# Decoder layer with two attentions on one core: full-width matmul pieces move ahead of the tiled ones in each attention step

## What is computed

```
x = layernorm(x + L0_attn(x))                    # 4 blocks of linear attention and feed-forward
x = layernorm(x + L0_xattn(x, ctx, mask))        # 16 heads of 8, masked softmax over 256 keys
x = layernorm(x + L0_ffn(x))
# L0_ffn: rmsnorm; rotary self-attention, 16 heads of 64, causal;
#         then one shared and 31 routed experts, the best 3 of 31 for each token
scores = where(mask, q k^T, -inf);  attn = softmax(scores);  ctx = attn @ v
```

## Time and profile before

| what | value |
| --- | --- |
| executions shown | 903.26, 904.5, 901.44 us |
| median | 903.26 us |
| span of the profiled execution, first to last instruction | 867.6 us |
| own time of the profiled execution | not shown apart; the median less the span is 35.7 us |
| TensorE busy | 796.4 us (92%), 5325 matmuls |
| VectorE busy | 692.1 us (80%) |
| ScalarE busy | 572.9 us (66%) |
| GpSimd busy | 562.2 us (65%) |
| mean granted TensorE clock | 0.982 |

### The profile page before, as it was taken

One profiled execution on the slowest core, in us unless ns is written; L12 is line 12 of the kernel. 1 busy time (PEld: TensorE's weight loads), 2 busy tenths in 40 slices (PEclk: granted clock), 3 DMA queues, 4 the chain that ended last, 5 costly groups with the idle time before them and its releaser, 6 DMA issues.

```text
span 867.6 us, 17391 instructions
## 1 busy us (share of the span) xinstructions
PE 796.4 (92%) x5325; PEld 525.5 (61%) x5325; DVE 692.1 (80%) x2494; ACT 572.9 (66%) x1445; POOL 562.2 (65%) x638
## 2 busy tenths in 40 slices
PE   5899999999889999999989999999999888989994
PEld 2344444444466676766546676676667556888773
DVE  4788888888788988889878859976995985565786
ACT  3588778777489999999656647645664656355334
POOL 4888888888662333232377749665788988663773
PEclk9799999999989999999999999999999999999997
DMA  8300000000015011100222222221222236264112
GB/s 242 116 2 0 1 1 0 1 0 1 0 36 153 30 42 56 39 1 2 50 65 68 65 50 51 68 65 40 63 76 77 54 93 195 91 191 146 50 49 61
DMA packets 57851, 51.88 MB, mean 60 GB/s; under 512 B 11586, under 2 KB 43042, under 8 KB 57762
## 3 DMA queue, kind: packets, MB, share of 16 engines
q1 hardware_dynamic: 55394, 46.05, 19.2%
q0 software_dynamic: 2304, 4.72, 1.9%
q10 hardware_dynamic: 64, 0.02, 0.0%
HBM read 21.66 MB, written 12.32 MB: 39 GB/s over the span
## 4 chain that ended last, share of the span: by engine, by line
PE 51%; POOL 19%; DVE 13%; issue 8%; ACT 7%; ACTq 0%; DVEq 0%; POOLq 0%
PE psum L2199 5%; PE psum L2028 4%; PE psum L2061 4%; POOL area L970 4%; DVE area L1482 4%; PE psum L2355 3%; PE psum L2336 3%; PE psum L2394 3%; PE psum L2258 3%; PE psum L2045 3%; POOL area L879 3%; PE psum L2087 3%; PE psum L2372 3%; POOL slot_in L958 2%; PE psum L1912 2%
## 5 line engine op out<-in xcount | busy, mean ns | idle before, releaser
L970 POOL TENSOR_TENSOR area<-area,rinv 128x512 f32<-128x512 f32 x64 | 94.2, 1472 | 64.7 <-DVE rinv L1803 64.3
L1275 ACT ACTIVATE area<-area,negmax 128x128 f32<-128x128 f32 (+1 forms) x256 | 112.8, 444 | 17.7 <-DVE negmax L1482 17.4
L1122 ACT ACTIVATE area<-area,negmax 128x256 f32<-128x256 f32 x256 | 108.9, 507 | 0.2
L1470 DVE SCALAR_TENSOR_TENSOR area<-psum,ccol,cs 128x512 f32<-128x512 f32 x128 | 89.4, 740 | 21.2 <-PE psum L2061 21.0
L1482 DVE CUSTOM_DVE_ANT_0 area<-psum,area 128x256 f32<-128x256 f32 x256 | 93.2, 420 | 14.4 <-PE psum L2013 13.9
L1482 DVE CUSTOM_DVE_ANT_0 area<-psum,maskc 128x128 f32<-128x128 f32 (+1 forms) x256 | 75.8, 351 | 10.0 <-PE psum L2087 10.0
L2028 PE MATMUL psum<-ident,area 128*128 128x128 f32 x512 | 70.9, 279 | 9.0 <-DVE area L1522 7.7
L2061 PE MATMUL psum<-area,qkw 128*128 128x512 f32 x128 | 71.9, 643 | 6.3 <-DVE area L1470 4.5
L2028 PEld LDWEIGHTS psum<-ident,area 128*128 128x128 f32 x512 | 57.3, 143 | 18.1 <-issue 11.3
L1265 ACT ACTIVATE area<-psum 128x512 f32<-128x512 f32 x32 | 19.1, 598 | 72.1 <-PE psum L2394 72.0
L2372 PEld LDWEIGHTS psum<-ident,area 128*128 128x128 f32 x384 | 44.8, 141 | 35.2 <-issue 24.9
(11 more groups left out here) (308 smaller groups left out, 2092.3 us busy)
## 6 DMA issues: line engine op xcount, KB each, us to landing
area<-area SPq DMA_DIRECT2D x256, 64.0 KB
slot_out<-area SPq DMA_DIRECT2D x17, 256.0 KB, 2.4
area<-slot_in SPq DMA_DIRECT2D x8, 512.0 KB, 4.0
slot_in<-gate SPq DMA_DIRECT2D x5, 768.0 KB, 4.6
area<-in_L_ffn_re_w SPq DMA_DIRECT2D x14, 256.0 KB, 3.4
area<-in_mask_BxSxS_ik SPq DMA_DIRECT2D x8, 256.0 KB, 3.8
area<-in_L_attn_W SPq DMA_DIRECT2D x5, 256.0 KB, 6.2
area<-in_x SPq DMA_DIRECT2D x4, 256.0 KB, 3.4
```

The costliest lines, as they stand in the source:

```text
L970: pool.tensor_tensor(p4, p4, rinv[:, u % 4, 0:4].unsqueeze(2).to_broadcast([128, 4, w]), ALU.mult)\
L1122: last = act.activation(P[:, n % 4, r, mm, :], P[:, n % 4, r, mm, :], ACT.Exp, bias=negmax[:, n % 4, r, mm:mm + 1], scale=-1.0)
L1275: last = act.activation(Pc[:, u % 4, r, mm, 0:w], Pc[:, u % 4, r, mm, 0:w], ACT.Exp, bias=negmax[:, u % 4, r, mm:mm + 1], scale=-1.0, accu ...
L1470: last = nc.vector.scalar_tensor_tensor(rp[:, w, j, :].rearrange("p (b n) -> p b n", b=2), src.rearrange("p (b n) -> p b n", b=2), ccol[:, ...
```

## The change: the order of three lists

On TensorE, in an odd step of the context attention, `values` moves from before the late and head pieces to the end of the step, so that the next step's scores come right behind. In a self-attention step the spare pieces move ahead of `self_scores`, so that `values` comes right behind the scores. On VectorE the reads of these spare pieces move ahead of `self_max` in the same way; the reads of `out`, `rank` and `base` stay behind it. ScalarE's, GpSimd's and SyncE's lists stay as they are, and no instruction is added or taken away. The hunks are VectorE's self-attention, TensorE's context attention and TensorE's self-attention.

```
@@ -1814,10 +1814,13 @@
                     if u == 1:
                         read_spare(g, steps[0], following)
+                    for step in steps:
+                        if step[0] in ("v", "logits", "pick", "b2") or step[0] == "tail" and step[1] in ("tokens0", "tokens1", "out"):
+                            read_spare(g, step, following)
                     if u < SU and (u + 2 < SU or following is not None):
                         self_max(g, u + 2)
                     for step in steps:
-                        if step[0] in ("v", "out", "logits", "rank", "base", "pick", "b2") or step[0] == "tail" and step[1] in ("tokens0", "tokens1", "out"):
+                        if step[0] in ("out", "rank", "base"):
                             read_spare(g, step, following)
@@ -2101,13 +2104,13 @@
-                if n % 2 and 0 <= n - 3 < XN:
-                    values((n - 3) // 2)
                 for what, b in fills(n, LATE):
                     fill_second(what, b)
                 for what, i in head(n):
                     pe.wait_ge(x_read, FILL[what, i])
                     fill_step(SPARE_FIRST[i], None, 0).then_inc(x_fill, 1)
+                if n % 2 and 0 <= n - 3 < XN:
+                    values((n - 3) // 2)
@@ -2411,11 +2414,11 @@
-                    if u < SU and (u + 2 < SU or following is not None):
-                        self_scores(g, u + 2)
                     for step in steps:
                         if step[0] not in ("half", "out", "rank", "base"):
                             fill_spare(g, step, following)
+                    if u < SU and (u + 2 < SU or following is not None):
+                        self_scores(g, u + 2)
                     if 2 <= u < SU + 2:
                         values(u - 2)
```

## The result

| | median, us | lowest to highest | runs |
| --- | --- | --- | --- |
| before | 903.89 | 899.74 to 908.75 | 22 |
| changed | 906.68 | 903.55 to 910.83 | 22 |

The changed kernel takes 1.0026 of the time before (95% interval 1.0013 to 1.0038): 2.3 us more by the ratio. It is slower, by little, though the interval lies clear of 1. The forecast, 898.1 us with a range to 904.0, is wrong in sign. The granted TensorE clock of the timed executions differs too: its mean is 0.962 for the 22 of the changed kernel, and 0.968 for 69 executions of before that stood beside later runs.

What follows compares the result with a forecast made beforehand. ScalarE was taken to bound mid context attention, TensorE the first self-attention group, VectorE the third. Terms -3.0 - 0.9 - 4.7 + 3.4 = -5.2 us, from 903.26, gave 898.1 us, 8-in-10 range 892.5 to 904.0.

Steps and rivals of the forecast that it cites:

- stage by stage reading: ScalarE fullest in mid context attention; self-attention: TensorE in first group (49.27 of 50 us), VectorE in third (47.87).
- reading of 35.7 us: Whole kernel: 35.7 us of a timed execution were taken to lie around the profiled span.
- Part 1: Middle context attention: `context` ahead of the values removes ScalarE's 1.00 us wait; 0.5 us a sequence, -3.0 us (0 to -6.0).
- Part 2: End of context attention: head pieces ahead of the values come 1.0 us earlier for VectorE; -0.9 us (0 to -1.2).
- Part 3: Self-attention: fewer tile-shape changes gain where TensorE is full; 2.2, 1.1, 1.0 and 0.4 by group, -4.7 us.
- price of a tile shape: TensorE, self-attention: each change of tile shape costs 0.19 us, and the new order saves one in a step.
- Part 4: Self-attention: a spare piece that waits now holds up the scores too; +3.4 us given back (0 to +5).
- rms: First self-attention group: this TensorE piece waits 0.73 us for GpSimd, with the scores now behind it; +0.55 us.
- turn: Router piece on TensorE, three groups: waits for VectorE's L1629 with the scores now behind; +0.6 us each, +1.9.
- gates: Second self-attention group: this TensorE piece waits for VectorE ahead of the scores; +0.35 us.
- logits: Router piece ahead of the scores, three groups: about 0.2 us absorbed in second and third, +0.6 in the last.
- VectorE waits for late scores: Rival, chance 0.10: self-attention `v` steps start scores 0.86 us later; 12 places costing that add 10.3 us, giving 908.

Runs made afterwards that it cites:

- context_only: Kernel before with only the context attention's part of the change: ratio 0.9969 to the kernel before, -2.7 us.
- v_heads_behind: Changed kernel with only `v` ahead in the self-attention, and the context attention's head pieces back behind the values: 902.78 us, ratio 0.9968 to before.
- turn_back: Changed kernel with the router's `turn` (three times) behind the scores again, on TensorE alone: ratio 0.9990 to before.
- unwaited_ahead: Changed kernel with `rms`, `turn`, `logits`, `gates` behind the scores again on TensorE, and `logits` behind the minima on VectorE: 901.51 us, ratio 0.9971 to before.
- v_only: Changed kernel with only `v` ahead in the self-attention, on TensorE and VectorE; context attention's part kept: 865.99 us, ratio 0.9953 to before, short chip.
- v_only_again: Same kernel as `v_only`, run again on the long chip: 901.3 us, ratio 0.9977 to before.
- after_again: The changed kernel run once more, nothing altered, on the long chip: 906.31 us, ratio 1.0024 to before.

## Why the prediction was wrong, step by step

The prediction failed in two steps: its gross gain, -8.6 us, was 3.9 too large (parts 1 to 3), and part 4 priced a wait only at the work that no longer hid in it.

**What bounds the kernel.** The stage by stage reading held, though the earlier trace rows, cited for the first group, are of the second. For the third group it says that what TensorE saves there doesn't count, and part 3 counts 1.0 us there all the same; the first was right. The reading of 35.7 us did not hold; it did no harm to the sum, which is a difference, but hid the fact that rows of a different chip were used.

**Part 1, right in mechanism, a third too large.** Forecast -3.0, 0.5 for each of six sequences. Measured over five sequences (from the third to the thirteenth L1144) 112.86 us against 114.68, 0.36 each, and -2.1 for the stage with its end. A sequence repeats every 22.57 us, above the 22.4 to 22.5 named as the sign of being right. The new wait on the values is 0.61 us; the prediction's own times (copy from 377.81, L1144 at 378.7) imply some 0.5, so 0.1 of the missing 0.14 lies there.

**Part 2, wrong.** Forecast -0.9, measured nothing from the heads, and from the thirteenth L1144 to the end of the stage 42.07 us against 41.80: +0.3, with +0.3 more in the next step. The failed step is "Ahead of them it comes 1.0 us earlier": VectorE's read of the half piece starts 31.3 us after the thirteenth L1144 in both orders, and its wait only shrinks from 1.92 to 1.81 us. In `context_only`, VectorE and then TensorE:

```profile
429.31 1.41 DVE L1470 SCALAR_TENSOR_TENSOR area<-psum,ccol,cs 128x512 f32<-128x512 f32 x2 [1.81 <-PE psum L2061]
```

```profile
428.14 1.13 PE L2061 MATMUL psum<-area,qkw 128*128 128x512 f32 x2 [0.82 <-ACT area L1110]
...
433.67 1.13 PE L2061 MATMUL psum<-area,qkw 128*128 128x512 f32 x2 [1.50 <-DVE area L1470]
```

The piece of the first row waits for ScalarE's copy in front of the values, and the next one for VectorE itself; the first starts 30.1 us after the thirteenth L1144 in both orders, the second 0.3 us later than before. The 0.3 us is not the heads' doing, for `v_heads_behind` has it too (42.14); what returns it was not tried.

**Part 3, gain of `v` right where TensorE is full, absent elsewhere.** The price of a tile shape was confirmed. A `v` step from the turn to the values, changed kernel and then before (short chip):

```profile
537.59 1.04 PE L2375 MATMUL psum<-ident,area 128*128 128x128 f32 x8
538.46 1.03 PE L2071 MATMUL psum<-vw,area 128*128 128x256 f32 x4
539.42 0.71 PE L2090 MATMUL psum<-area 64*128 64x128 f32 x8
540.07 0.66 PE L2397 MATMUL psum<-area 128*64 128x128 f32 x8
```
```profile
538.70 1.04 PE L2372 MATMUL psum<-ident,area 128*128 128x128 f32 x8
539.66 0.71 PE L2087 MATMUL psum<-area 64*128 64x128 f32 x8
540.31 1.13 PE L2068 MATMUL psum<-vw,area 128*128 128x256 f32 x4
541.37 0.66 PE L2394 MATMUL psum<-area 128*64 128x128 f32 x8
```

2.48 us instead of 2.67, so 0.19 saved as forecast, though L2071 itself takes 0.96 and not 0.87: the turn in front of it, 0.87 instead of 0.96, has the other tenth. Half of the 0.19 is the weight load, as the prediction had it: in before the first load of L2068 starts 0.11 us ahead of its product behind a full-width piece (425.96 and 426.07 us), and with it behind scores. The second group gains 1.0 us with `v` alone (forecast 1.1), the first 1.0 behind its second step, 1.65 with the tail pieces (forecast 2.2). The third gains 0.2 (forecast 1.0), and the last none (0.4). That is 2.9 of 4.7.

**Part 4, the step that failed.** The give-backs were forecast at +3.4. The step is the pricing of `rms` ("The scores (0.65 us) stood in front and now stand behind: +0.55") and, in the same way, of `turn` (+0.6 each). Measured: `rms` 0.7 without and 2.2 with the dip; `turn` 1.2 in each of two groups; `gates` in the second group 0.5 without a dip (forecast 0.35; `turn_back` against `unwaited_ahead`, from the tenth step to the twelfth) and 1.6 more with one (77.41 less 75.82). `logits` ahead, forecast at nothing in the second and third group, gains 0.2 in each (for instance `turn_back` 39.07, `v_only` 39.27). In the last group `turn` waits 2.12 us instead of 1.48, and a dip follows in all four profiles with `turn` ahead, but in two of the ten others as well (`v_only`, `v_heads_behind`). That group still takes 62.2 to 63.0 us from its second step, against 62.15, so all that stands ahead there gives back 0 to 0.8, where `turn` and `logits` were forecast at some 1.3.

```profile
694.27 1.09 PE L2246 MATMUL psum<-ident,rT 128*128 128x128 f32 x4 [2.12 <-DVE rT L1629]
695.29 1.23 PE L2090 MATMUL psum<-area 64*128 64x128 f32 x8
696.45 1.12 PE L2397 MATMUL psum<-area 128*64 128x128 f32 x8
697.50 2.08 PE L2064 MATMUL psum<-area,qkw 128*128 128x512 f32 x2
```

Each wait was priced at the work that no longer hid in it. Two things stood in no term. The longer idle stretch can be followed by 3.4 us at half clock, 1.2 to 1.6 us more. And a delay of tenths turned into one of 0.8 us through an overlap of VectorE and GpSimd; the prediction names such a shift beside its third rival (L1629, L1707), but counts nothing for it.

**The sum.** Context -2.1 + 0.3; `v`, `out` and tail pieces -2.9; `rms`, `turn`, `gates` +0.7 + 2.4 + 0.5 = +3.6; `logits` -0.4; together -1.5 up to the end of the third group, without a dip. So part 4's +3.4 came out near its size, but by luck: `turn` cost twice its price, `logits` gained, and the last group gave back less. Both profiles of the changed kernel have two dips in this part, +1.2 to 1.6 each, and end at +1.6 and +1.3 by the table; the last group adds 0 to 0.5; the runs say +2.3. Of the 7.5 us between forecast and result 3.9 are gains that did not come and some 3 are half-clock stretches. That the dips are not only in the profiles shows in the timed executions on the long chip. Their mean granted clock is 0.968 for before (69 executions), 0.962 and 0.963 for the changed kernel (22 and 12), 0.965 for `turn_back`, and 0.966 for `v_only_again` and `unwaited_ahead` (12 each). My estimate from these means and a span of 905 us is 8 to 10 us more at half clock for the changed kernel, two to three stretches of 3.4 us. At 1.2 to 1.6 us each they add 2.9 to 4.7 us to the -1.5, and the 2.3 of the runs lies between.

**The rivals.** "VectorE waits for late scores" (chance 0.10) had the right sign and the wrong place: with VectorE's own order changed along, the `v` steps cost nothing, and that its 908 us lies near the 906.7 measured is luck. No rival held the longer idle of TensorE and its clock. The forecast's own range, too, doesn't follow from its terms: parts 1 and 4 halfway to their bounds give 894.9 to 900.4, not 894.5 to 901.0.

## What to carry to other kernels

In a list that one engine runs in order, work that never waits can be moved for the sake of tile shapes; a piece that waits for another engine should keep behind it what is not yet due and ahead of it what is ready, since ready work in front hides the wait. Split such a change by whether the piece waits: here the part without waits (`v_only`, 0.9953 and 0.9977; `unwaited_ahead`, 0.9971) beats both kernels, and the whole lost. Price a grown wait at more than the work that no longer hides in it: ask also what the delay will run into on the other engines, and look at the granted clock behind it in several profiles. And before rows of one profile are added up against timed runs, compare its own time with theirs.

## What the runs showed of the hardware

- Two chips run this kernel at 870 and 904 us. On the longer one ScalarE's L1265 waits 8.2 us at the start of the last group, where it waits 4.7 on the shorter one, and L1253 waits 23.2 us in the experts with a releaser the profile can't name. No run shows what it is.
- Half-clock stretches come in some executions and not in others of the same order. In the first three groups (without the first step) they came only behind a wait of TensorE of 1.3 to 2.6 us: the fourteen profiles hold fifteen such waits, and a stretch follows eight of them; the eight profiles without such a wait have none. At `rms` three of four waits of 1.76 to 1.79 us were followed by one, and none of ten waits of 0.72 to 1.61 us. At 441 us four of the ten profiles with the context attention's part have one, and none of the other four, though TensorE waits 1.58 us there in all fourteen. One such stretch turns L2064 from 1.13 into 2.08 us.
- A VectorE instruction on SBUF alone (L1707) takes 0.29 us when no GpSimd instruction runs at its start (`after_again`, 703.94 us). Started 0.3 us before the end of L801 it takes 0.43 us, and started under L802 1.17 us: both times it ends 0.14 us behind the GpSimd instruction under which it started. In the last group of before, started under L970, it takes 3.43 us, until L801 and L802 behind that are done too.
- The cost of a change of tile shape stands in the row before it as well as in the one behind: a turn takes 0.87 us in front of full-width work and 0.96 in front of 64-row tiles.
